# A four-layer network on one core: a joined stage that leaves its outputs by pixels and sums them on GpSimd, a Fourier layer that turns no rows, and another order at the opening

## The reference, cut to what matters

```python
# x: (4, 512, 64, 64)
x = x + L0(_gn(x))      # layer 0: a learned recurrence over 4096 tokens in chunks of 16
x = x + L1(_gn(x))      # layer 1: rfft2, a two-layer complex product per frequency, irfft2
x = x + L2(_gn(x))      # layer 2: a gate per channel from block means
x = x + L3(_gn(x))      # layer 3: as layer 1

def step(carry, inp):   # layer 0, per chunk and head, 256 chunks in sequence
    W1c, b1c = carry
    xq, xk, xv, et = inp
    Z1 = xk @ W1c + b1c
    grad = _ln_l2_bwd(Z1, xv - xk, g, bb)
    Attn1 = jnp.tril(xq @ xk.swapaxes(-1, -2))
    b1_bar = b1c - jnp.tril(et) @ grad
    Z1_bar = xq @ W1c - et * Attn1 @ grad + b1_bar
    last_eta = et[..., -1, :, None]
    W1n = W1c - (last_eta * xk).swapaxes(-1, -2) @ grad
    b1n = b1c - (last_eta * grad).sum(-2, keepdims=True)
    return ((W1n, b1n), xq + _ln(Z1_bar, g, bb, EPS_IN))
# ... then  _ln(out, post_w, post_b, EPS_IN) @ o_w.T
```

## Time and profile before

| | us |
|---|---|
| median of 3 runs | 5496.47 (5491.76 to 5501.12) |
| the profiled execution | 5496.87 |
| its span | 5494.8 |
| opening, from the start to DVE's last instruction of it | 82.2 |
| project, to the last store issued | about 1548 |
| scan_and_read, to DVE's last bn_aggr | 3811 |
| first Fourier layer | about 3820 to 4650 |
| second Fourier layer | about 4760 to the end |

### The profile page before, as it was taken

How to read it: one execution, slowest core, us unless ns; L and a number is a source line. 1 busy time by engine, 2 the same in 40 slices (tenths; PEclk the granted TensorE clock), 3 DMA queues, 4 the chain that set the end, 5 groups by cost and what they waited for, 6 DMA issues and landing times. The chain is left out here.

```text
span 5494.8 us, 134571 instructions
## 1 busy us (share of the span) xinstructions
PE 5182.9 (94%) x44534; PEld 3981.5 (72%) x44534; DVE 4161.1 (76%) x14714; ACT 2608.8 (47%) x7573; POOL 2700.2 (49%) x4382
## 2 busy tenths in 40 slices
PE   5999999999969999999999999997999997799998
PEld 2444444444438888888888888886899986699998
DVE  4766667656558888888888888885888888566665
ACT  0111111111136777777777777773555554454454
POOL 1444444444436666666666666662454443333332
PEclk8999999999969999999999999998999999899999
DMA  4434444433324444444444444443122211221221
GB/s 185 167 121 156 152 139 152 136 124 126 128 88 121 129 127 126 127 127 130 127 127 127 128 127 128 126 128 132 75 94 79 94 79 49 90 94 78 86 87 78
DMA packets 599449, 644.80 MB, mean 117 GB/s; under 512 B 172980, under 2 KB 503100, under 8 KB 587868
## 3 DMA queue, kind: packets, MB, share of 16 engines
q1 hardware_dynamic: 440844, 491.84, 27.7%
q10 hardware_dynamic: 157904, 144.22, 7.8%
HBM read 357.96 MB, written 278.00 MB: 116 GB/s over the span
## 5 line engine op out<-in xcount | busy, mean ns | idle before, releaser
L1592 PE MATMUL proj_ps<-proj_w_sb,proj_h 128*128 128x512 f32 x3072 | 1345.2, 596 | 0.0
L1592 PEld LDWEIGHTS proj_ps<-proj_w_sb,proj_h 128*128 128x128 f32 x3072 | 576.6, 190 | 741.3 <-issue 722.4
L1495 DVE SCALAR_TENSOR_TENSOR proj_lin<-proj_ps,proj_rstd,proj_wbias_sb 128x512 f32<-128x512 f32 x384 | 283.4, 746 | 493.9 <-PE proj_ps L1592 488.3
L1900 POOL TENSOR_TENSOR scan_b_step<-scan_core,scan_rate_last 128x128 f32<-128x128 f32 x512 | 327.6, 640 | 595.0 <-DVE scan_core L2160 595.0
L2369 PE MATMUL scan_ps_y<-scan_o_t,proj_wo_sb 128*128 128x128 f32 x4096 | 566.2, 281 | 2.1 <-ACT scan_o_t L2003 2.1
L2369 PEld LDWEIGHTS scan_ps_y<-scan_o_t,proj_wo_sb 128*128 128x128 f32 x4096 | 496.7, 191 | 32.3 <-ACT scan_o_t L2003 2.6
L1410 POOL TENSOR_TENSOR proj_gk<-proj_rec,proj_gain_sb 128x256 f32<-128x256 f32 x256 | 181.2, 728 | 528.4 <-DVE proj_rec L1516 528.4
L1969 ACT ACTIVATE scan_square<-scan_ps_z 128x64 f32<-128x64 f32 x1024 | 219.1, 219 | 461.1 <-PE scan_ps_z L2288 457.4
L1404 POOL TENSOR_TENSOR proj_by_cos<-proj_lin,proj_rope 128x512 f32<-128x512 f32 x256 | 335.7, 1325 | 162.7 <-DVE proj_lin L1495 121.0
L2300 PE MATMUL scan_ps_w<-scan_step,scan_record 64*128 64x128 f32 x4088 | 354.2, 293 | 13.3 <-DVE scan_step L2165 12.3
L1962 ACT COPY scan_state_w<-scan_ps_w 128x512 f32<-128x512 f32 x480 | 278.7, 581 | 123.3 <-PE scan_ps_w L2300 122.2
(11 more groups left out here) (326 smaller groups left out, 13189.2 us busy)
## 6 DMA issues: line engine op xcount, KB each, us to landing
scan_record<-records SPq DMA_DIRECT2D x259, 392.0 KB
records<-proj_rec ACTq DMA_DIRECT2D x256, 392.0 KB, 3.8
spectra<-fourier_spec SPq DMA_DIRECT2D x16, 2112.0 KB, 6.4
fourier_spec<-spectra SPq DMA_DIRECT2D x16, 2112.0 KB, 8.5
proj_h<-x SPq DMA_DIRECT2D x32, 1024.0 KB, 6.4
queries<-proj_q ACTq DMA_DIRECT2D x128, 256.0 KB, 3.8
gradients<-scan_stored SPq DMA_DIRECT2D x512, 64.0 KB
scan_q_in<-queries SPq DMA_DIRECT2D x128, 256.0 KB, 7.8
```

The source lines that it names most:

```text
L1495: v.scalar_tensor_tensor(lin[q][:, n], ps[q][n][:], rstd[k][:, j:j + 1], T.wbias[:, n], ALU.mult, ALU.add).then_inc(lin_sb.sem, 1)
L1592: last = pe.matmul(ps[j % 2][n][:], h[k][:, ct, j * P:(j + 1) * P], T.w[:, n, ct], start=ct == 0, stop=ct == CT - 1)
L1900: v.tensor_tensor(b_step[g][:], core[g][:], rate_last[g][:, :, 2:3].broadcast_to([P, PB, HD]), ALU.mult).then_inc(b_step_sb[g].sem, 1)
```

## The change

In the opening SP waits for the small loads, then loads weights and image tiles alternately; DVE takes the statistics of tile 0, the rate weights, projection 0, tile 1, projection 1, tiles 2 and 3, projection 2. The output bias is made as a row of 512 in every partition, by four matmuls of 512 columns instead of 16 sums of one column. The scan's constants are loaded in the opening and made on DVE at project's start (`scan_constants`).

In the scan the output projection has the turned outputs standing and the weights moving (one matmul of 512 columns a quarter, and one with the image tile standing and the identity moving); its result is by pixels. DVE's `leave` adds the bias, in even steps; ACT squares the tile in the next odd step; POOL adds the tile and its squares to running sums (`totals`), at the end of every odd step. DVE's bn_stats and bn_aggr are gone; 32 one-column matmuls sum over pixels at the end. x1 is stored by pixels, in runs of 2 KB rather than 512 B.

In fourier_forth the units are read by pixels, so that the rows are transformed straight from the loaded tile, with no turn and no copy. ACT copies the transformed columns, and DVE makes 13 box sums in the column phase and 19 in the mix phase; ACT's energy sums all move to the mix phase.

```diff
@@ scan_and_read, POOL
+            def totals(tile):
+                t, b, sc, par, half = tile
+                pool.wait_ge(y_done.sem, y_done.at(t, 1))
+                if sc:
+                    pool.wait_ge(total_sb.sem, total_sb.at(t - 3, 0))
+                v.tensor_tensor(total[:, b, 0], total[:, b, 0], y_sb[par][:, b], ALU.add).then_inc(total_sb.sem, 1)
+                pool.wait_ge(y_sq_sb.sem, y_sq_sb.at(t, 1))
+                v.tensor_tensor(total[:, b, 1], total[:, b, 1], y_sq[t % 2][:], ALU.add).then_inc(total_sb.sem, 1)
...
-                if at.odd and at.tile(OUT):
-                    shifted(at.tile(OUT))
+                if at.odd:
+                    if at.tile(OUT):
+                        shifted(at.tile(OUT))
+                    if at.tile(LEAVE):
+                        totals(at.tile(LEAVE))
@@ scan_and_read, ACT
-            def leave(tile):
...
-                for n in range(CT):
-                    done = a.activation(y_sb[par][:, b * CT + n], ps_y[:, n], ACT.Identity, bias=T.wo_bias[:, n:n + 1])
-                done.then_inc(y_done.sem, 1)
+            def output_tile_squares(tile):
...
+                a.activation(y_sq[t % 2][:], y_sb[par][:, b], ACT.Square).then_inc(y_sq_sb.sem, 1)
...
                     if norm:
                         output_root(norm)
+                    if gone:
+                        output_tile_squares(gone)
                 else:
-                    if gone:
-                        leave(gone)
@@ scan_and_read, DVE
-            def moments(tile):
+            def leave(tile):
                 t, b, sc, par, half = tile
-                dve.wait_ge(y_done.sem, y_done.at(t, 1))
-                for n in range(CT):
-                    where = stats6[:, b * CT + n, bass.ds(sc, 1), :].rearrange("p o e -> p (o e)")
-                    v.bn_stats(where, y_sb[par][:, b * CT + n]).then_inc(stats_sb.sem, 1)
+                dve.wait_ge(y_ps.sem, y_ps.at(t, 1))
...
+                v.tensor_tensor(y_sb[par][:, b], ps_y[:], T.wo_bias[:], ALU.add).then_inc(y_done.sem, 1)
...
-                    if gone:
-                        moments(gone)
...
-                elif norm:
-                    outputs(norm)
+                else:
+                    if gone:
+                        leave(gone)
+                    if norm:
+                        outputs(norm)
...
-            dve.wait_ge(stats_sb.sem, stats_sb.at(TILES, 0))
-            for u in range(UNITS):
-                v.bn_aggr(chan_stats[:, u, :], stats6[:, u].rearrange("p s e -> p (s e)"))
+            dve.wait_ge(means_ps.sem, means_ps.at(0, 1))
@@ scan_and_read, PE, tile_project
-                for ct in range(CT):
-                    pe.matmul(ps_y[:, n], T.wo[:, ct, n * P:(n + 1) * P], o_t[:, ct], start=ct == 0, stop=False)
+                pe.matmul(ps_y[:], o_t[:, n], T.wo[:, n], start=n == 0, stop=n == CT - 1, skip_group_check=True)
...
-                done = pe.matmul(ps_y[:, n], T.ident[:], x_sb[par][:, b * CT + n], start=False, stop=True)
+                done = pe.matmul(ps_y[:, n * P:(n + 1) * P], x_sb[par][:, b * CT + n], T.ident[:], start=False, stop=n == CT - 1,
+                                 skip_group_check=True)
@@ opening, SP and DVE
+            sp.wait_ge(small_in, 16 * small_loads)
+            for n in range(CT):
+                if n < 3:
+                    sp.dma_start(T.w[:, n], d["wT"][n]).then_inc(w_in[n], 16)
+                sp.dma_start(xb[n][:], x_view[n]).then_inc(x_in_sb[n], 16)
...
             statistics(0)
-            statistics(1)
...
             projection(0)
+            statistics(1)
+            projection(1)
             statistics(2)
             statistics(3)
@@ project, DVE
             v.memset(rec_sb[:], 0.0).then_inc(init.sem, 1)
             dve.wait_ge(init.sem, init.at(0, 1))
+            scan_constants()
@@ fourier_forth
+                act.wait_ge(box_sb.sem, box_sb.at(u, 0))
+                evacuate(u, 0, packed[0][1] * P)
+                for n, (s, m) in enumerate(slots):
+                    evacuate(u, n + 1, packed[n + 1][1] * P if n + 1 < NB2 else 2 * P)
+                    act.wait_ge(dft_ps.sem, dft_ps.at(u, PRE + n + 1))
+                    nc.scalar.copy(spec[k][:, s:s + m].rearrange("p s r h -> p (s r h)"), psD[n % 2][:, 0:m * P]).then_inc(col_sb.sem, 1)
...
+                dve.wait_ge(prod_sb.sem, prod_sb.at(u, 0))
+                boxed = 13
+                for g in range(boxed):
+                    box_of_last(u, 1 - k, g)
...
-            def turn_rows(u, i, k):
-                transposes(u, ROW + i, [xb[k][:, (4 * i + j) * P:(4 * i + j + 1) * P] for j in range(4)])
+            def rows(u, t, k, i):
+                for j in range(4):
+                    done = pe.matmul(psD[t % 2][:, j * P:(j + 1) * P], xb[k][:, 4 * i + j], F1, start=True, stop=True)
+                done.then_inc(dft_ps.sem, 1)
```

More of the change, by code:

```diff
@@ L155, in sig @@
             return Signal(ctx, nc, f"{name}_{n}", per, credit)
-        xb = [sb(f"x{k}", [P, TOK]) for k in range(2)]
+        xb = [sb(f"x{k}", [P, TOK // P, P]) for k in range(2)]
         wt = sb("weights", [P, CT, 4, P])
@@ L553, in transform_rows @@
                     pe.wait_ge(row_sb.sem, row_sb.at(u, NB1 + i - 1))
-                transforms(u, ROW + i, [(j * P, j, F1) for j in range(4)])
+                rows(u, ROW + i, k, i)
             def turn_columns(u, n):
@@ L611, in unit @@
                     mix1(u, k, ct, c)
-                    if not last:
-                        turn_rows(u, c, 1 - k)
                 for c in range(NCH):
@@ L625, in _ @@
             pe.wait_ge(x_loaded[0].sem, x_loaded[0].at(0, 16))
-            for i in range(NB1 + 1):
-                if i < NB1:
-                    transposes(0, i - PRE, [xb[0][:, (4 * i + j) * P:(4 * i + j + 1) * P] for j in range(4)])
-                if i > 2:
-                    pe.wait_ge(row_sb.sem, row_sb.at(0, i - 2))
-                if i:
-                    transforms(0, i - 1 - PRE, [(j * P, j, F1) for j in range(4)])
+            for i in range(NB1):
+                if i >= 2:
+                    pe.wait_ge(row_sb.sem, row_sb.at(0, i - 1))
+                rows(0, i - PRE, 0, i)
             pe.wait_ge(combined.sem, combined.at(0, 2 * CT))
@@ L1190, in _, with project @@
             pe.wait_ge(var_made, 1)
-            for ot in range(CT):
-                for ct in range(CT):
-                    last = pe.matmul(ps_small[:, 2, ot:ot + 1], T.wo[:, ct, ot * P:(ot + 1) * P], vecs[:, 3, ct:ct + 1],
-                                     start=ct == 0, stop=ct == CT - 1)
+            for ct in range(CT):
+                last = pe.matmul(ps_bias[0][:], vecs[:, 3, ct:ct + 1].broadcast_to([P, P]), T.wo[:, ct], start=ct == 0, stop=ct == CT - 1)
             last.then_inc(wo_folded, 1)
-def project(nc, T, x_in, rope, group_mean, gn_now, rec, q_out, images=B, groups=TOK // 512):
+def project(nc, T, K, x_in, rope, group_mean, gn_now, rec, q_out, images=B, groups=TOK // 512):
     x_view = x_in.rearrange("b (k c) h w -> b c k (h w)", c=P)
@@ L1679, in scan_and_read @@
         x_sb = [sb(f"x_in{q}", [P, UNITS, P]) for q in range(2)]
-        y_sb = [sb(f"y{q}", [P, UNITS, P]) for q in range(2)]
+        y_sb = [sb(f"y{q}", [P, B, C]) for q in range(2)]
+        y_sq = [sb(f"y_sq{q}", [P, C]) for q in range(2)]
+        total = sb("total", [P, B, 2, C])
+        mean_of = sb("mean_of", [P, 1])
+        chan_mean_sq = sb("chan_mean_sq", [P, UNITS])
         q_t = sb("q_t", [P, HP, P])
@@ L1773, in scan_and_read @@
         y_done = one("y_done")
-        stats_sb = one("stats_sb", CT)
+        y_sq_sb = one("y_sq_sb")
+        cleared = one("cleared")
+        total_sb = one("total_sb", 2)
+        mean_made = one("mean_made")
+        means_ps = one("means_ps")
         block = ctx.enter_context(nc.Block())
-        loads = 13
         class Place:
@@ L2420, in _ @@
             loop(pe, body)
+            pe.wait_ge(total_sb.sem, total_sb.at(TILES, 0))
+            pe.wait_ge(y_done.sem, y_done.at(TILES, 0))
+            pe.wait_ge(mean_made.sem, mean_made.at(0, 1))
+            for b in range(B):
+                for ct in range(CT):
+                    for e in range(2):
+                        n = (b * CT + ct) * 2 + e
+                        done = pe.matmul(ps_y[:, n:n + 1], total[:, b, e, ct * P:(ct + 1) * P], mean_of[:], start=True, stop=True)
+            done.then_inc(means_ps.sem, 1)
 def norm_factors(nc, name, gmean, grstd, gstd, gn, coef):
@@ L2581, in __init__, with sb @@
         self.pick = sb("pick", [P, NH + 2], until_projected)
+class ScanConstants:
+    loads = 13
+    def __init__(self, ctx, nc):
+        def sb(n, shape):
+            return ctx.enter_context(nc.sbuf_tensor(f"scan_{n}", shape, F32))
+        self.gain8 = sb("gain8", [P, HD])
+        self.eps = sb("eps", [P, 1])
+        self.tok_in = sb("tok_in", [P, 2])
+        self.last = sb("last", [P, 1])
```

(18 more changed lines are left out.)

237 lines of the change are left out of this document (99 added, 138 removed).

## The result

| | before | after |
|---|---|---|
| median, us | 5495.65 (5491.76 to 5501.12, 4 runs) | 5709.13 (5703.84 to 5721.69, 4 runs) |
| ratio | | 1.0391, 95% interval 1.0372 to 1.0410 |
| span of the profiled execution | 5494.8 | 5708.3 |
| mean granted clock of PE | 0.978 | 0.960 |

What follows compares the result with a forecast made beforehand. Prediction: PE and DVE are full, with POOL on a short leash between them; +288 us in the scan and -85 elsewhere give +203 on 5496.5, so 5700 us; range 5616 to 5772, or 5510 to 5780 with most of the queue-only rival.

Steps and rivals of the forecast that it cites:

- The ports, +2.3 us on the step: Scan, even step: POOL's two totals hold DVE's two-SBUF-operand t_row at shared ports, so the step starts 2.3 us later.
- 2.4 us a tile, 288 us: Scan: net cost on DVE's path per tile, over the 120 tiles with totals beside the recurrence.
- rival C: Scan: dearer, +3.5 us a tile, through PE's clock falling or later instructions meeting the totals' tail; 5832 us; 8%.
- zgain meets t_row once the bn_stats are gone, +0.7: Scan, group 1: DVE reaches t_row earlier and scan_zgain holds the ports, giving back 0.7 of the 0.8 us saved.
- The queue: Scan: POOL's totals delay the next step's rate, making DVE's step 1.5 us late, counted inside the 2.3 us.
- PE waits some 2 to 3 us a tile for the step: Scan: expected sign in the profile, PE waiting 2 to 3 us a tile for scan_step.
- PE's quarter: Scan, output projection: a quarter takes 1.12 instead of 1.21 us, saving PE about 0.4 to 0.5 us a tile.
- rival B: Scan: PE sets the tile, POOL's totals fit its gaps, 0.5 us a tile is won; 5352 us; 7%.
- The opening, -18: Opening: DVE's work ends near 64 us with the reordered loads, gaining 18 us (10 to 21).
- The prologue, -17: Scan's prologue: with the constants moved away, PE's start at 1578.43 comes 17 us earlier.
- The scan's end, -4: Scan's end: 14.22 us of bn_aggr go, one-column matmuls and waits of perhaps 10 come; ends -8 and +4.
- The Fourier layer, -42: First Fourier layer: dropping the turns of rows gains 2.8 us a unit (1.5 to 3.5) over 15 units.

Runs made afterwards that it cites:

- run 2: The change with GpSimd's two running sums cut into four pieces of 256 columns, placed where POOL waits for DVE's core: 5674.2 us, ratio 1.0320.
- Run 3: The change with DVE's zg, xh and cx kept in PSUM (free columns of ps_z) instead of SBUF, sums left in place: 5515.3 us, ratio 1.0037.
- run 4: The change with both edits, sums in four pieces in GpSimd's gaps and zg, xh, cx in PSUM: 5439.7 us, ratio 0.9899 to the kernel before.
- Run 8: The change with the scan's constants still loaded in the opening but made by DVE in the scan's prologue: 5706.7 us.

## Why the prediction was right, and where it was off

The total was 5700 forecast, 5709 measured, by the mechanism that it named. That it came within 9 us is luck in part: the scan's tiles were put 19 us too dear, and project's 16 us were not in the sum at all.

DVE's path through one tile, from step to step, shows which terms held (us, in the tiles shown, at full clock). Before, the steps start at 2500.44, 2504.69, 2509.04, 2513.77 and 2517.26; after, at 2505.40, 2508.90, 2513.09, 2517.43 and 2524.05. The last column has the prediction's terms for that stretch:

| to the step of | before | after | difference | forecast |
|---|---|---|---|---|
| even step, group 1 | 3.49 | 3.50 | +0.01 | 0 |
| odd step, group 0 (bias sum in, wait for the square out) | 4.25 | 4.19 | -0.06 | +0.6 - 0.4 |
| odd step, group 1 (bn_stats out, `scan_zgain` met) | 4.35 | 4.34 | -0.01 | -0.8 + 0.7 |
| even step, group 0 (the two totals) | 4.73 | 6.62 | +1.89 | +2.3 |
| the tile | 16.82 | 18.65 | +1.83 | +2.4 |

- *The ports, +2.3 us on the step.* Right in kind, shown by runs 2 and 3: DVE's instructions with two SBUF operands are held for the rest of GpSimd's, those with one in PSUM are not. From step(1) of the odd step to the next step it was 4.73 us; after, from 2517.43 to 2524.05, 6.62. The hold is 2.36 - 0.47 = 1.9 us, not 2.3. POOL's instructions of 512 columns follow each other every 1.23 us, where I had taken 1.37: 0.3 us for two. And the second `scan_t_row` ends 0.1 us behind the total that holds it, as the 1.31 us row did, where I had let it start there: the other 0.1.
- *2.4 us a tile, 288 us.* Mean 19.18 - 16.94 = 2.24 us a tile, and 268 us for the stage with its tail. The tiles away from any fall of the clock take 18.68, 1.74 more than before. The other 0.5 is a part that the prediction had given to rival C: the granted clock was 0.96 in the change's scan (windows above) and 1.00 in that of the kernel before. So one term was too large, and a mechanism that I had set apart as a rival was there at a part of its price.
- *zgain meets t_row once the bn_stats are gone, +0.7.* Seen, 0.93 instead of 0.57 us: +0.4. Yet nothing is left of the bn_stats' 0.8 us on that stretch: the two terms made -0.1 together, the table has -0.01. What took the rest I did not follow.
- *The bias sum, 0.6 us.* 0.60 to the next start.
- *The queue.* Said to be inside the ports' part, 1.5 us late. Right as far as run 2 shows: with the ports' part there, taking the queue's away shortens no tile at full clock (18.85 against 18.68), though its pieces also meet DVE's instructions more often. Run 3 shows it by itself: 1.19 us of wait, and 17.51 against run 4's 16.71 us a tile. Taking away the ports' part alone won 194 us; the queue's, once the ports' was gone, another 76.
- *PE waits some 2 to 3 us a tile for the step.* Less. The view of PE's waits from 1700 to 3900 us, where some 115 tiles lie, has 0.75 us a tile for `scan_step` and 0.27 for `scan_y`, which was not forecast:

```profile
PE scan_ps_w L2295 <- DVE scan_step L2155: 86.5, 146, 1.3
PE scan_ps_y L2364 <- DVE scan_y L2165: 31.4, 81, 0.7
```

- *PE's quarter, 1.12 instead of 1.21.* Wrong: from 2515.90 to 2517.08 it is 1.18 (and 1.25 from 2510.07 to 2511.32). Two loads of weights instead of five saved 0.03, not 0.1: I had taken 0.24 us for the identity's matmul, and it costs 0.32 (2516.76 to 2517.08; before, 2508.77 to 2509.09). That is why rival B could not have given 5352 us: in run 4, where POOL's price is gone, the tile is 16.71 in the median, 0.1 below before, and in the mean the same 16.94.
- *The opening, -18.* -21: the small loads were there at 7.88 us, not at 12.
- *The prologue, -17.* -12.8. I had put PE's start 13.8 us behind project's end, and it came 18.4 behind it. Run 8 shows that DVE's instructions were not part of what goes: they are free behind the records' load, which PE waits for in any case. The wait for 13 loads was the price.
- *The constants in project, 0.* No cost shown (run 8). But project's +16 was not in the sum at all, and its cause stays open.
- *The scan's end, -4.* +3 (36.6 us from the last `scan_zgain` to the stage's end, 33.8 before): 64 passes of 0.22 us make 13.8, for 14.2 of bn_aggr, and POOL's last two sums stand ahead of them. I had taken 10. PE waits 3.34 us ahead of these passes (row above), and the windows view has its clock at 0.50 throughout them.
- *The Fourier layer, -42.* -34 from first to last product, 2.3 a unit: inside the range given (1.5 to 3.5). Box sums, which read two tiles in SBUF, are held in the same way (mean 0.71 instead of 0.60 us a box): in both kernels those of 256 columns that start while GpSimd runs an instruction take 1.0 to 1.1 us and the others 0.63, and 195 of 306 start so after the change, 144 before. How much of the missing 0.5 us a unit is theirs no run separates.

## What to carry to other kernels

Work given to GpSimd because it is idle on average is paid where it stands: once in its queue, by whoever waits for the next small instruction behind it, and once at the ports, by each VectorE instruction with two SBUF operands that meets it. The larger price can hide the smaller. Take both away before judging: with the sums moved into GpSimd's waits alone the kernel is 178 us slower than before, with operands in PSUM alone 19 slower, and with both 56 us faster. Follow one period on all engines first; the share of busy time said that GpSimd had 870 us to spare.
